# Attention: maxima subtracted on GpSimd for four heads at once, and one exponential of 512 columns in place of four of 128

## What is computed

```python
def _L0_xattn_ref(q, k, v, start_pos, mask):
    N_HEADS = 32
    N_KV_HEADS = 8
    HEAD_DIM = 16
    scores = jnp.einsum('bsgrd,btgd->bgrst', xq, xk) / math.sqrt(HEAD_DIM)
    scores = scores + mask
    probs = jax.nn.softmax(scores.astype(jnp.float32), axis=-1).astype(q.dtype)
    out = jnp.einsum('bgrst,btgd->bsgrd', probs, xv)
    return out.reshape(b, s, N_HEADS * HEAD_DIM)

x = _layernorm(x + _L0_xattn_ref(x, ctx_1024, ctx_1024, 0, mask_SxS2_ff0), axis=-1)
```

## Time and profile before

| what | value |
|---|---|
| median of 3 runs | 1687.86 us |
| profiled execution | 1687.67 us, span of instructions 1685.9 us |
| TensorE busy over the span | 96% |
| VectorE, ScalarE, GpSimd busy over the span | 70%, 56%, 56% |
| attention stage, first scores to first hidden (L1320) | 1413.3 to 1529.1 us |
| granted TensorE clock over the span | 0.989 of full |

### The profile page before, as it was taken

One profiled execution on the slowest core, in us unless ns is written; L12 is line 12 of the kernel. 1 busy time (PEld: TensorE's weight loads), 2 busy tenths in 40 slices (PEclk: granted clock), 3 DMA queues, 4 the chain that ended last, 5 costly groups with the idle time before them and its releaser, 6 DMA issues.

```text
span 1685.9 us, 25533 instructions
## 1 busy us (share of the span) xinstructions
PE 1625.2 (96%) x9160; PEld 1278.2 (76%) x9160; DVE 1179.1 (70%) x2257; ACT 948.9 (56%) x1577; POOL 947.3 (56%) x716
## 2 busy tenths in 40 slices
PE   6899999999999999999999999999999978889998
PEld 4788888888888888888888888888888865444646
DVE  4785858685868586858684868486848668896443
ACT  3583648364837383738373847384738354995231
POOL 3594839483949294929493949395929562231000
PEclk8999999999999999999999999999999989999999
DMA  5241224131423142313231323142314181001000
GB/s 206 71 136 58 99 66 135 63 101 59 135 70 101 57 132 76 101 57 132 76 100 57 132 71 105 52 135 62 115 45 137 63 139 57 1 11 29 13 13 25
DMA packets 76546, 138.84 MB, mean 82 GB/s; under 512 B 6786, under 2 KB 13954, under 8 KB 76164
## 3 DMA queue, kind: packets, MB, share of 16 engines
q1 hardware_dynamic: 76420, 137.21, 25.9%
HBM read 134.55 MB, written 2.63 MB: 81 GB/s over the span
## 4 chain that ended last, share of the span: by engine, by line
PE 90%; DVE 5%; ACT 2%; issue 1%; DMA 1%; SPq 1%; POOL 0%; DVEq 0%; ACTq 0%
PE ps_hs L246 8%; PE ps_hs L248 8%; PE ps_hs L247 8%; PE ps_gate L246 8%; PE ps_gate L248 8%; PE ps_gate L247 8%; PE ps_y L1123 7%; PE ps_hs L1131 7%; PE ps_hs L1133 7%; PE ps_hs L1132 7%; PE ps_gate L1112 4%; PE ps_y L1358 3%; PE ps_hs L1320 3%; PE ps_dec L1320 3%; DVE pr L959 1%
## 5 line engine op out<-in xcount | busy, mean ns | idle before, releaser
L750 DVE SCALAR_TENSOR_TENSOR conv<-ps_hs,cw,conv 128x508 f32<-128x508 f32 (+2 forms) x432 | 320.3, 742 | 30.7 <-ACT conv L511 19.6
L378 POOL TENSOR_SCALAR_AFFINE_SELECT cum_bc<-cum_bc 128x1024 f32<-128x1024 f32 x128 | 140.1, 1095 | 238.9 <-DMA cum_bc<-cum_scratch 238.2
L388 POOL TENSOR_TENSOR cum_bc<-cum_bc,neg_cum 128x1024 f32<-128x1024 f32 x128 | 247.7, 1936 | 23.1 <-DVE neg_cum L855 12.6
L246 PE MATMUL ps_hs<-x_hi,w_hi 128*128 128x512 f32 x576 | 232.6, 404 | 7.8 <-DVE conv L750 7.8
L248 PE MATMUL ps_hs<-x_hi,w_lo 128*128 128x512 f32 x576 | 225.8, 392 | 0.0
L247 PE MATMUL ps_hs<-x_lo,w_hi 128*128 128x512 f32 x576 | 225.0, 391 | 0.0
L246 PE MATMUL ps_gate<-x_hi,w_hi 128*128 128x512 f32 x576 | 224.7, 390 | 0.0
L247 PE MATMUL ps_gate<-x_lo,w_hi 128*128 128x512 f32 x576 | 224.3, 389 | 0.0
L248 PE MATMUL ps_gate<-x_hi,w_lo 128*128 128x512 f32 x576 | 224.3, 389 | 0.0
L1131 PE MATMUL ps_hs<-wo_hi,g_hi 128*128 128x512 f32 x512 | 202.6, 396 | 8.4 <-DVE acc L924 6.4
L1133 PE MATMUL ps_hs<-wo_hi,g_lo 128*128 128x512 f32 x512 | 200.7, 392 | 0.0
(11 more groups left out here) (142 smaller groups left out, 3140.0 us busy)
## 6 DMA issues: line engine op xcount, KB each, us to landing
cum_bc<-cum_scratch SPq DMA_DIRECT2D x128, 512.0 KB, 4.2
w_raw<-w_in SPq DMA_DIRECT2D x145, 256.0 KB, 4.6
wo_raw<-w_out SPq DMA_DIRECT2D x64, 256.0 KB, 5.0
g_acc<-x_t SPq DMA_DIRECT2D x4, 512.0 KB, 6.5
acc<-x_nat SPq DMA_DIRECT2D x1, 2048.0 KB, 9.3
k_rep<-ctx_t SPq DMA_DIRECT2D x8, 256.0 KB, 11.1
out<-y_out SPq DMA_DIRECT2D x8, 256.0 KB, 2.0
wg_sb<-w_gate SPq DMA_DIRECT2D x1, 1792.0 KB, 12.4
```

The costliest lines, as they stand in the source:

```text
L246: eng.matmul(ps, whi, xhi, start=(k == 0), stop=False)
L388: gp.tensor_tensor(part, part, start.broadcast_to([P, 2, HB, SEQ]), ALU.add).then_inc(S["bc_ok"], 1)
L750: v.scalar_tensor_tensor(out=dst, in0=src, scalar=cw[:, at, TAPS - 1 - n:TAPS - n], in1=dst, op0=ALU.mult, op1=ALU.add).then_inc(S["tap"], 1)
```

## The change

GpSimd, in place of the loop over L461 alone, first spreads the keys of chunks 0 and 1. Then for each chunk it waits for each half's minima (s_max), subtracts them from the half's 128 x 512 negated scores in place (broadcast along the columns), raises a new semaphore p_sub, and after both halves spreads the keys of chunk i + 2. ScalarE waits for p_sub in place of s_max and takes one exponential of 128 x 512 a half, without a bias.

```diff
-            for i in range(CHUNKS):
+            def spread_keys(i):
+
                 need(pool, S["s_ps"], 2 * i - 2)
                 gp.tensor_tensor(k_bd[i % 2][:, :, :],
                                  k_rep[:, i // KD, i % KD, :].unsqueeze(1).broadcast_to([P, REP, SEQ]),
                                  kbd_mask[:, 0, :].unsqueeze(2).broadcast_to([P, REP, SEQ]),
                                  ALU.mult).then_inc(S["kbd_ok"], 1)
+
+            spread_keys(0)
+            spread_keys(1)
+            for i in range(CHUNKS):
+                for par in range(2):
+                    pool.wait_ge(S["s_max"], 2 * i + par + 1)
+                    four = slice(par * REP, (par + 1) * REP)
+                    gp.tensor_tensor(pr[i % 3][:, four, :], pr[i % 3][:, four, :],
+                                     neg_max[:, i % 3, four].unsqueeze(2).broadcast_to([P, REP, SEQ]),
+                                     ALU.subtract).then_inc(S["p_sub"], 1)
+                if i + 2 < CHUNKS:
+                    spread_keys(i + 2)
@@
             def exponentials(i, par):
 
-                act.wait_ge(S["s_max"], 2 * i + par + 1)
-                for r in range(REP):
-                    n = par * REP + r
-                    e = sc.activation(pr[i % 3][:, n, :], pr[i % 3][:, n, :], ACT.Exp, scale=-1.0,
-                                      bias=neg_max[:, i % 3, n:n + 1])
-                e.then_inc(S["p_exp"], 1)
+                act.wait_ge(S["p_sub"], 2 * i + par + 1)
+                part = pr[i % 3][:, par * REP:(par + 1) * REP, :]
+                sc.activation(part, part, ACT.Exp, scale=-1.0).then_inc(S["p_exp"], 1)
```

More of the change, by code:

```diff
@@ L210, in build @@
             "st1", "mv1", "var1", "root1", "inv1", "x1_ok", "q_ps", "q_sb",
-            "s_ps", "s_max", "p_exp", "pt_ps", "pt_a", "pt_v", "pv_ps", "pvs_ok", "back_ps", "rec_ok", "att_ok",
+            "s_ps", "s_max", "p_sub", "p_exp", "pt_ps", "pt_a", "pt_v", "pv_ps", "pvs_ok", "back_ps", "rec_ok", "att_ok",
             "xa_ok", "st2", "mv2", "var2", "root2", "inv2", "x2_ok", "x2_tr", "x2_hi_ok", "x2_lo_ok",
```

## The result

The changed kernel takes 1719.3 us (median of 4 runs, 1718.65 to 1721.11), the kernel before 1688.5 us beside it. The ratio is 1.0184, with a 95% interval of 1.0166 to 1.0202. I had forecast slower, 1706 us with 1715 as the upper end: the direction was right, and the size was missed by 13 us, outside the range. The profiled execution has a span of 1716.9 us, 31.0 more than before.

What follows compares the result with a forecast made beforehand. The prediction took VectorE's work and, in every other pair, a TensorE-VectorE loop as the bound. It added 11.5 us (ten pairs) and 7.0 us (first chunks), together 18.5, to 1687.67 us: 1706 us, range 1699 to 1715.

Steps and rivals of the forecast that it cites:

- What bounds the kernel: Attention's middle: VectorE's work holds half the pairs, a TensorE-VectorE loop the others; two chunks take 6.97 us.
- The loop through the late keys: Attention: keys queued behind GpSimd's subtractions delay scores, transposes and the next minima; 8.10 us a pair before the clash.
- M: M(i) is the time at which VectorE has the minima of chunk i; M(i + 2) was put at M(i) + 8.10.
- The first chunks: Attention's first eight chunks, up to M(8): 1445.9 in place of 1438.94, +7.0 us.
- The ten pairs: Attention from M(8) to M(28), ten pairs of chunks at 8.3 us: 83.0 us in place of 71.5, +11.5 us.
- The rest of the stage: From M(28) to the first hidden matmul: the same steps as before, 18.7 us.
- The clash: GpSimd and VectorE taking turns on two-operand SBUF reads, the residual sum delaying the key spread: 0.2 us a pair, 0 to 0.45.
- the second part of the sum: In the loop, from scores(i + 2) to M(i + 2): 3.19 us to kt and 2.29 us to the minima, as before.
- the clock as a rival at 9%: Attention: TensorE's idle time lowers its clock, half of the pairs losing 1.5 us, plus 5 for the ends: 1721 us, 9%.
- a clock below 1.00 in the stage: Sign that the forecast is wrong: TensorE's granted clock in the attention stage leaves 1.00.
- No change or faster: Two rivals: no change through slack in the middle, about 1688 us, 5%; faster because ScalarE was the bound, 1677 us, 6%.
- a gain from ScalarE: Rival: ScalarE was the bound, so first scores to first hidden matmul shrink by 10.9 us, to 1677 us; 6%.

Runs made afterwards that it cites:

- e4: Kernel before with one exponential of 512 columns a half in place of four, and no subtraction of the maxima: 1688.2 us, ratio 0.9992.
- e1: Changed kernel with the keys of chunk i + 2 spread ahead of the two subtractions of chunk i: 1695.8 us, ratio 1.0029.
- e5: Kernel before, exponentials untouched, with two spare GpSimd operations behind each chunk's minima and the key spread of chunk i + 2 behind them: 1725.7 us, ratio 1.0205.
- e3: Changed kernel with filler matmuls of 128x512 on TensorE while it waits for the keys: 1709.4 us, ratio 1.0115.
- e6: Changed kernel with keys first, and GpSimd's second subtraction in certain chunks waiting for VectorE's residual sum or norm: 1691.1 us, ratio 1.0003.

## Why the prediction was right in kind and short in size

**What bounds the kernel.** Right. I took ScalarE's 95% for a load beside the path, and e4 confirms it for the middle: with 16 us of 50 taken off it, the pairs gain 0.07 us each in the mean. I expected ScalarE idle for a third of the time afterwards, and it was idle for 27.9 of 50 us, and GpSimd was busy for 66% and not over 70%: both do the same work for fewer chunks in that time.

**The loop through the late keys.** Right in its steps and their sizes. Subtractions of 1.04 us, keys at M + 2.54 (2.47 in the working), scores at M + 2.64 (2.62), M to M 8.12 us (8.10). e1 removes it by moving two lines, e5 brings it about without the rest of the change.

**The first chunks.** +7.0 us in the working, +7.1 in e3 where the clock is held, +10.5 in the kernel itself. **The ten pairs.** +11.5 us in the working, +10.6 in e3, +21.0 in the kernel itself. **The rest of the stage.** Unchanged, as I had it.

**The clash.** Its price on the loop was 0.2 us a pair between 0 and 0.45. The spread is indeed stretched, from 1.04 to 1.22 us, but a pair at full clock is no longer than the sum without it, since the pairs' other terms came out as small as that. I put no price on the other side, VectorE's: its residual sum grows from 0.42 to 0.89 us. In the changed kernel that is hidden by VectorE's waiting; with the keys first it isn't, and costs 4 us in ten pairs (75.3 for 71.4 in e6). The Trainium skill (SBUF — State Buffer, "SBUF: two separate sides") says the loser of the shared ports fully blocks. The trace agrees in kind: the sum in e1 ended 0.29 us behind GpSimd's subtraction. That is less than its own 0.42 us, so the trace doesn't show that it stood still the whole time.

**The step that failed** is the second part of the sum, where TensorE's 3.19 us from scores to kt were carried over from a kernel in which TensorE hardly waits. In the slow pairs they are longer, 4.83 us from M(14) to M(16). I had the clock as a rival at 9% (1721 us, for half of the pairs) and left it out of the range, though I named a clock below 1.00 in the stage as a sign that the forecast is wrong. What I set against it was one stretch, 1420 to 1424 us, with TensorE busy for 2.40 of 4 us at a clock of 1.00. That stretch was held up as a share of busy time. What came was lumps (that they are what lowers the clock is my reading, and no run varied the wait alone): in the trace of the changed kernel TensorE waits 2.3 to 2.5 us at one go before the scores of chunks 12, 16, 20 and 24, where the kernel before waited 1.22 us at most in the middle of the stage, and all four of these pairs are slow. In the kernel before it was behind a wait of 2.11 us, at 1523 us in its timeline, that the clock fell to 0.57. That row was the better witness, if not a sure one: the changed kernel has a wait of 2.21 us at 1555 us with nothing slow behind it. The clock costs at least 3.4 us in the first chunks (10.5 less 7.1) and 10.4 in the pairs (21.0 less 10.6), together 13.8 of the 31.4 us. The rival's price of 1.5 us was near the 1.6 that a slow pair shows, and all that the rival gave to the clock was 14.8 us (9.8 for pairs and 5 for the ends). Its parts partly cancel: seven in ten pairs were slow, not five, and the ends lost 3.4 and not 5. I had given it too small a chance to let it into the range.

**No change or faster.** Neither rival held. For a gain from ScalarE I had a price of 11 us; e4 found 2.8 us of stage and no measurable time.

## What to carry to other kernels

When work is added to an idle engine, ask what already stands in that engine's queue behind it, and follow who waits for that: here two operations put ahead of a third on the least busy engine closed a loop over all of them, and moving two lines undid most of it. A wait put in front of TensorE has to be priced twice, as the wait and as slower matmuls behind it, and the second can be nearly as large as the first (here 14 us beside 18). Relieving the busiest engine brought no measurable time here until work from the path was moved onto it.

## What the runs showed of the hardware

TensorE's clock went to its lower level for a part of seven pairs in ten, though the engine was busy for 37.9 of 50 us; with useless matmuls in the gaps it stayed at the higher level up to M(28), and the kernel was 10 us faster. Of the waits before the scores, all four of 2.3 to 2.5 us were followed by matmuls at the lower level, and three of six of about 1.2 us; in the kernel before, waits of 1.22 us were followed by none. The same wait of 2.21 us near the end of the stage was followed by the lower level in e3 and by none in the changed kernel. So one wait by itself doesn't decide it, and what does wasn't tried.

A VectorE sum with both operands in SBUF (128 x 256, 0.42 us) took up to 1.35 us beside subtractions on GpSimd (e1), and VectorE's masked instructions, with one operand in PSUM, kept their 0.28 us beside the same ones. Letting GpSimd wait until the sum was done (e6) took 4.8 us off the stage of e1, 4.0 of them in the ten pairs.
